# Another order for the mask work of a gated cross-attention block: vector engine, GpSimd and loads

## The reference

```python
q_in  = layernorm(x)
query = layernorm(q_in @ Wq + bq)            # 2 x 2048 x 512, 16 heads of 32
key, value = layernorm(ctx @ Wk + bk), layernorm(ctx @ Wv + bv)
scores = einsum('bhqd,bhkd->bhqk', query, key) / sqrt(32)
scores = where(mask[:, None] == 0, -1e9, scores)      # mask: 2 x 2048 x 154, int32
out = softmax(scores) @ value
x = x + tanh(g_xattn[1]) * (out @ Wo + bo)
```

## Time and profile before

| what | us |
|---|---|
| median of 3 runs | 2475.44 (2474.05 to 2477.65) |
| the profiled execution, its span from first to last instruction | 2475.2 |
| TensorE busy | 2414.1 (98%) |
| VectorE busy | 1444.5 (58%) |
| ScalarE busy | 1087.0 (44%) |
| GpSimd busy | 245.9 (10%) |
| DMA | 147.27 MB, mean 59 GB/s |

### The profile page before, as it was taken

How to read it: one execution, slowest core, us unless ns; L and a number is a source line. 1 busy time by engine, 2 the same in 40 slices (tenths; PEclk the granted TensorE clock), 3 DMA queues, 4 the chain that set the end, 5 groups by cost and what they waited for, 6 DMA issues and landing times.

```text
span 2475.2 us, 33128 instructions
## 1 busy us (share of the span) xinstructions
PE 2414.1 (98%) x13344; PEld 1826.1 (74%) x13344; DVE 1444.5 (58%) x2410; ACT 1087.0 (44%) x1762; POOL 245.9 (10%) x223
## 2 busy tenths in 40 slices
PE   6999999999999999999989999999999999999998
PEld 5666667688888888888755666666778888888886
DVE  5555566542222222222666666665888888888986
ACT  4343433442222222223334333334666666666665
POOL 2021112210000000000301111112000000000000
PEclk9999999999999999999999999999999999999999
DMA  3121111421101100102311222223501101101000
GB/s 126 35 86 52 52 52 69 158 85 52 52 1 52 51 18 35 51 18 85 113 58 61 78 78 78 78 73 102 167 18 35 52 18 48 38 20 49 35 30 22
DMA packets 92600, 147.27 MB, mean 59 GB/s; under 512 B 5408, under 2 KB 28320, under 8 KB 92448
## 3 DMA queue, kind: packets, MB, share of 16 engines
q1 hardware_dynamic: 92448, 145.16, 17.4%
HBM read 111.59 MB, written 33.55 MB: 59 GB/s over the span
## 4 chain that ended last, share of the span: by engine, by line
PE 40%; DVE 8%; ACT 2%; issue 1%; DMA 0%; POOL 0%; SPq 0%; DVEq 0%; ACTq 0%
PE l_lay_bank L69 18%; PE l_lay_score L69 11%; PE l_lay_values L1493 1%; PE l_lay_score L1416 1%; PE l_lay_score L1418 1%; PE l_lay_score L1468 1%; PE l_lay_values L1497 1%; PE l_lay_sums L1505 1%; DVE l_at_at_next L1036 1%; DVE l_at_h_lo L1050 1%; DVE l_at_at_next L1029 1%; DVE l_at_full L1025 1%; DVE l_at_full L1018 1%; DVE l_at_xTf_lo L924 1%; PE l_lay_bank L1339 1%
## 5 line engine op out<-in xcount | busy, mean ns | idle before, releaser
L69 PE MATMUL l_lay_score<-l_at_tw_hi,l_at_h_hi 128*128 128x512 f32 x1024 | 401.5, 392 | 5.2 <-DVE l_at_h_lo L1050 4.7
L69 PE MATMUL l_lay_bank<-l_at_xTf_hi,l_at_tw_hi 128*128 128x512 f32 x1024 | 400.0, 391 | 0.0
L69 PE MATMUL l_lay_score<-l_at_tw_hi,l_at_h_lo 128*128 128x512 f32 x1024 | 398.7, 389 | 0.0
L69 PE MATMUL l_lay_score<-l_at_tw_lo,l_at_h_hi 128*128 128x512 f32 x1024 | 398.5, 389 | 0.0
L69 PE MATMUL l_lay_bank<-l_at_xTf_hi,l_at_tw_lo 128*128 128x512 f32 x1024 | 398.4, 389 | 0.0
L69 PE MATMUL l_lay_bank<-l_at_xTf_lo,l_at_tw_hi 128*128 128x512 f32 x1024 | 398.4, 389 | 0.0
L1010 DVE TENSOR_TENSOR l_at_h_lo<-l_at_full,l_at_h_hi 128x512 fp32r<-128x512 f32 x128 | 99.6, 779 | 466.0 <-ACT l_at_h_hi L740 466.0
L735 ACT ACTIVATE l_at_full<-l_lay_bank,l_at_lay_b 128x512 f32<-128x512 f32 x128 | 88.4, 690 | 457.5 <-PE l_lay_bank L69 457.5
L69 PEld LDWEIGHTS l_lay_score<-l_at_tw_hi,l_at_h_hi 128*128 128x128 f32 x1024 | 192.2, 188 | 49.2 <-DVE l_at_h_lo L1050 10.3
L69 PEld LDWEIGHTS l_lay_score<-l_at_tw_hi,l_at_h_lo 128*128 128x128 f32 x1024 | 192.2, 188 | 40.3
L69 PEld LDWEIGHTS l_lay_bank<-l_at_xTf_hi,l_at_tw_lo 128*128 128x128 f32 x1024 | 192.2, 188 | 40.0
(11 more groups left out here) (224 smaller groups left out, 4078.9 us busy)
## 6 DMA issues: line engine op xcount, KB each, us to landing
both_x_in<-stream SPq DMA_DIRECT2D x25, 1024.0 KB, 5.6
l_at_xg<-stream SPq DMA_DIRECT2D x23, 1024.0 KB, 5.5
stream<-l_at_xg SPq DMA_DIRECT2D x22, 1024.0 KB, 4.3
l_at_tw_raw<-in_l_w SPq DMA_DIRECT2D x64, 256.0 KB, 5.6
l_at_maskT_in<-in_maskT SPq DMA_DIRECT2D x40, 256.0 KB, 2.6
both_x_in<-in_x SPq DMA_DIRECT2D x9, 1024.0 KB, 7.6
l_at_xg<-in_x SPq DMA_DIRECT2D x7, 1024.0 KB, 5.3
out<-l_at_xg SPq DMA_DIRECT2D x7, 1024.0 KB, 4.3
```

The lines of the kernel that those rows point to most:

```text
L69: done = nc.tensor.matmul(out, lhs[a], rhs[b], start=first and n == 0, stop=last and n == len(passes) - 1)
```

## The change

Only code under `norm`, that is layer 1, runs in another order; no instruction is added or removed. On VectorE, pieces 1 to 4 of chunk `it` are converted at the head of iteration `it` itself (1 and 2 between the halves of `xT_front`, 3 and 4 after `recip_of`), `mask_front` goes ahead of the query rows, piece 0 of the next chunk and the input norm between the query rows, the query norm directly behind its statistics, and `qT_front` one step later each. GpSimd takes `x_rstd_of` ahead of `q_rstd_of`. SP issues pieces 3 and 4 of chunk `it` at the start of iteration `it`, then the input, pieces 0 and 1 of the next chunk, the other mask, and piece 2. In the loops TensorE's and ScalarE's programs are as before.

```diff
--- before.py
+++ after.py
@@ -450,17 +450,20 @@
                 load_maskT(1, 0)
                 load_maskT(1, 1)
             for it in range(NCH):
+                if norm and it:
+                    load_maskT(it, 3)
+                    load_maskT(it, 4)
                 if it < last:
                     load(it + 2)
                 else:
                     load_last_residual()
-                if norm and it + 2 < NCH:
-                    load_masks(it + 2)
+                if norm and it:
+                    load_maskT(it + 1, 0)
+                    load_maskT(it + 1, 1)
                 if norm:
-                    for i in range(2, PIECES):
-                        load_maskT(it + 1, i)
-                    load_maskT(it + 2, 0)
-                    load_maskT(it + 2, 1)
+                    if it + 2 < NCH:
+                        load_masks(it + 2)
+                    load_maskT(it + 1, 2)
                 if it == last - 1:
                     weights(0)
                     weights(1)
@@ -588,10 +591,10 @@
                     add_bias(it - 1, gate_bias)
                 if it == last:
                     add_bias(last, gate_bias)
+                if it < last:
+                    x_rstd_of(it + 2)
                 if norm and it < last:
                     q_rstd_of(it + 1)
-                if it < last:
-                    x_rstd_of(it + 2)
                 if it:
                     widen(it - 1, range(RB, KT))
                 if it == last - 1:
@@ -1182,39 +1185,43 @@
                     if m in (8, 15):
                         kv_evict(6 + m // 15)
             for it in range(last):
-                xT_front(it + 1)
+                xT_front(it + 1, (0, 1))
+                if norm and it:
+                    maskT_front(it, 1)
+                    maskT_front(it, 2)
+                xT_front(it + 1, (2, 3))
                 if it:
                     recip_of(it - 1)
                 else:
                     k_lo_of(1)
-                for half in ((0, 1), (2, 3)):
-                    if norm:
-                        q_rows_front(it + 1, half)
-                    else:
-                        q_front(it + 1, half)
-                    if not norm and half[0] == 0:
-                        norm_stats(it + 2)
                 if norm:
+                    if it:
+                        maskT_front(it, 3)
+                        maskT_front(it, 4)
+                    mask_front(it + 1)
+                    q_rows_front(it + 1, (0, 1))
+                    maskT_front(it + 1, 0)
+                    norm_stats(it + 2)
+                    q_rows_front(it + 1, (2,))
+                    norm_apply(it + 2)
+                    q_rows_front(it + 1, (3,))
                     q_norm_stats(it + 1)
-                    norm_stats(it + 2)
                     q_norm_apply(it + 1)
                 else:
+                    q_front(it + 1, (0, 1))
+                    norm_stats(it + 2)
+                    q_front(it + 1, (2, 3))
                     norm_apply(it + 2)
                 if it:
                     c_back(it - 1, (0, 1))
                 if norm:
-                    mask_front(it + 1)
-                    maskT_front(it + 1, 0)
-                    norm_apply(it + 2)
-                    qT_front(it + 1, (0, 1))
+                    qT_front(it + 1, (0,))
                 if it:
                     c_back(it - 1, (2, 3))
                 for m in range(NM):
                     max_of(it + 1, m)
-                    if m in (2, 3) and norm:
-                        qT_front(it + 1, (m,))
-                    if m in (4, 6, 10, 13) and norm:
-                        maskT_front(it + 1, {4: 1, 6: 2, 10: 3, 13: 4}[m])
+                    if m in (1, 3, 5) and norm:
+                        qT_front(it + 1, ((m + 1) // 2,))
                     if it and m in (7, 11, 14):
                         y_back(it - 1, (m - 6) // 4)
                 if it:
@@ -1224,8 +1231,15 @@
                         v_normalise(2)
                         v_normalise(3)
                     front.take_lo(dve, "wd")
-            xT_front(NCH)
+            xT_front(NCH, (0, 1))
+            if norm:
+                maskT_front(last, 1)
+                maskT_front(last, 2)
+            xT_front(NCH, (2, 3))
             recip_of(last - 1)
+            if norm:
+                maskT_front(last, 3)
+                maskT_front(last, 4)
             for u in range(2):
                 if norm:
                     round_hidden(u)
```

## The result

| | before | after |
|---|---|---|
| median, us | 2474.74 (2473.79 to 2477.65, 4 runs) | 2538.55 (2537.29 to 2539.91, 4 runs) |
| ratio | | 1.0252 [1.0239, 1.0265] |
| profiled execution: span, us | 2475.2 | 2536.8 |
| TensorE's mean granted clock | 0.993 | 0.98 |

The changed kernel is 63.8 us slower. The forecast was 2533.0 (2492 to 2546), its likeliest case with a chance of 0.74; the median lies 5.6 us over it and inside the range. In the code after the change the same steps stand on other lines: the conversions on L919, `scores_main`'s first matmul on L1489, the maxima on L974 (VectorE) and L1430 and L1432 (TensorE), `qT_front`'s transposes on L1409, `add_bias` on L542.

A forecast was written before the change was run, and what follows sets the result against it. TensorE was taken to set the loop's pace. To the profiled span of 2475.2 us came 47.2 of mask waits and 11.9 of clock, less 1.35 at chunk 0: 2533.0 us, range 2492 to 2546.

The forecast's parts named there:

- likeliest case: Layer 1's chunks: mask pieces land behind the residual and `add_bias` delays their conversions; 2516 to 2545 us, chance 0.74.
- The loads behind the residual: SP, start of each iteration: pieces 3 and 4 land about 0.7 and 1.4 us behind the 1 MB residual.
- the hold: VectorE's conversion of piece 3 is held until GpSimd's running `add_bias` (4.6 us) ends; TensorE goes on 0.75 us later.
- the queue: Late landing behind the residual, conversions still 0.41 us: waits of 18.1 us; as a rival 2492 to 2504 us, chance 0.13.
- The rival of the overtaking pieces: Pieces 3 and 4 land after 2.6 us, before the residual; only chunk 1 waits, 2.2 us: 2476 us, chance 0.08.
- Chunk by chunk: TensorE's waits for the masks in chunks 1 to 7: 9.3, three of 4.7, two of 6.85, and 10.1 us.
- the second hold: Chunk 7: another `add_bias` follows at once and takes the ports between the two conversions; wait 10.1 us, otherwise 5.4.
- The clock: TensorE's clock falls once behind each of the 7 waits, 1.7 us each: 11.9 us, bounds 0 and twice that.
- VectorE's part: VectorE's new order in layer 1: 1.35 us gained at the end of chunk 0, nothing from its other moves.
- the first term: Four conversions leave the maxima loop of iteration 0, so TensorE gains 4 x 0.34 = 1.35 us.
- VectorE sets the pace: In the maxima loop of iteration 0 VectorE is the limit, so removing four conversions there saves TensorE 1.35 us.
- The sum: 2475.2 + 47.2 of waits - 1.35 at chunk 0 + 11.9 of clock = 2533.0 us.

The follow-up runs named there:

- experiment 2: The changed kernel with GpSimd's `add_bias` waiting until all masks of the chunk are converted, loads still behind the residual: 2501.18 us, ratio 1.0107.
- the swap alone: The kernel before with only GpSimd's `x_rstd_of` put ahead of `q_rstd_of`, VectorE's order unchanged: 2509.39 us, ratio 1.0131; 2509.74 us in a second set.
- experiment 1: The changed kernel with the next chunk's pieces 3 and 4 issued between the store and the residual load: 2476.14 us, ratio 1.0000.

## Why the prediction was right

**The loads behind the residual.** Right. The prediction had the pieces about 0.7 and 1.4 us behind the residual's landing. In chunk 1 the residual took 5.4 us from 1324.01 and the second piece 5.8 us from about 1324.9, 1.3 us behind it. With the hold gone the queue cost 17.4 us where 18.1 was worked out. The rival of the overtaking pieces fell: they would have landed after 2.6 us, and came ahead of the residual only once they were issued first (after 2.7 to 4.9 us). The chunks followed each other 69.3 to 76.3 us apart, where 67 and more was forecast.
The rule of the Trainium skill ("DMA: Bandwidth & Descriptors", "Queues, rings and completion order") that completion is not first in, first out gives no order; in these rows it was the order of issue.

**The hold.** Right, and the step with the least ground under it: one conversion of 1.34 us. The value taken, a hold to the end of `add_bias`, was the measured one: pairs of 4.47 to 4.50 us, and 4.15 us for the first conversion of chunk 7 where 0.41 is its own length. That it is `add_bias` that holds them is what experiment 2 shows.
The Trainium skill's exemption for one input in SBUF ("SBUF — State Buffer", "Who interferes with whom") did not apply to this instruction: 4.15 us. The same section names `tensor_scalar` among the operations that can enter a two-port mode, which the exemption leaves out. The rows fit that but don't prove it: the one from PSUM at 1763.26, of as many columns, takes 0.74 us, the conversion from SBUF 0.41.

**Chunk by chunk.** Forecast and measured waits: 9.3 and 8.95; 4.7 three times, and 4.80, 4.75, 5.17; 6.85 twice, and 6.57, 6.21; 10.1 and 10.95 with the second hold. The sum was 47.2 against 47.4. That the delay moves the next store and residual with it, so that the wait recurs, is what the seven rows show. The totals agree better than the parts, which is luck: chunk 7 is 0.85 over, and chunks 5 and 6 are 0.9 under. In chunk 7 the first `add_bias` began 1.5 us behind the place where TensorE needed the masks, not 0.1 as in the kernel before, and the second one took 4.67 us, not 5.04.

**The clock.** The mechanism was right, one fall at each of the seven waits, its size too small: 11.9 us forecast as 1.7 us a wait, 18.0 measured, within the bound of 23.8. Since the falls ahead of the waits are two here and three before, the clock term grew by 16.6 only; the prediction had no term for that. The 1.7 came from the fall behind a wait of 1.3 us; behind waits of 4.75 to 10.95 us it cost 1.6 to 3.3 us.

**VectorE's part.** "Nothing" held for everything but the first term. The four conversions that leave the loop over the maxima of chunk 0 were to give 1.35 us. VectorE's timeline of that loop after the change (first, the two places where it now stands idle, and what follows the loop):

```profile
1301.05 1.51 DVE L974 TENSOR_REDUCE l_at_maxes<-l_lay_score 128x4 f32<-128x616 f32 x2 [3.41 <-PE l_lay_score L1432]
...
1306.78 3.13 DVE L974 TENSOR_REDUCE l_at_maxes<-l_lay_score 128x4 f32<-128x616 f32 x4 [0.20 <-PE l_lay_score L1432]
1310.11 3.14 DVE L974 TENSOR_REDUCE l_at_maxes<-l_lay_score 128x4 f32<-128x616 f32 x4 [0.19 <-PE l_lay_score L1432]
1313.15 0.74 DVE L1109 SCALAR_TENSOR_TENSOR l_at_v_main<-l_at_v_main,l_at_lay_kv_mv,l_at_v_rows 128x512 f32<-128x512 f32 x1
```

The stretch takes 12.10 us, 12.86 before: a gain of 0.76. Without the conversions VectorE catches up with TensorE and waits 0.20 and 0.19 us for it, and the wait ahead of the first maxima grew from 1.3 to 1.8 us. The step that failed is "VectorE sets the pace": it did so only by a little.

**The sum.** Its start was off by chance. In all 97 executions here that have both numbers, the time lies 1.7 to 1.9 us over the span. So the profiled execution of before, with its span of 2475.2, took about 2477.0 us (an estimate), 2.3 over its median, and the 0.2 us between span and median were a coincidence. From the median instead, 2474.7 + 47.4 + 16.6 - 0.8 = 2537.9, 0.6 us short of the measured one. The 5.6 us between forecast and result are then -0.5 for the start, +0.2 for the waits, +4.7 for the clock, +0.6 for chunk 0, and 0.6 that are in no term.

## What to carry to other kernels

When a load is moved, look at what is issued just ahead of it on its queue, and at what starts on the other engines when that lands: here a residual of 1 MB was both the transfer in front and the trigger of the instruction that held the conversion. A small load with a near deadline goes ahead of the large one, into the time in which the queue waits anyway. Price each new wait of an otherwise busy TensorE at its length and, for waits from 3.4 us up as here, 1.6 to 3.3 us of clock on top, and treat a swap on a helper engine as free only together with the producer's order that it follows.

## What the runs showed of the hardware

- A conversion from int32 to bfloat16 with one input in SBUF was held by GpSimd's running instruction to its end (4.15 us in place of 0.41; without that instruction, beside the same transfers, 0.43 in experiment 2). Beside two GpSimd instructions back to back one conversion ended 0.3 us behind each: 4.15 and 4.71 us, 8.78 for the two.
- The clock's cost did not grow in step with the wait: behind six waits of 3.38 us (the swap alone) the falls cost 1.7 to 2.9 us each, 15.6 together; behind seven of 4.75 to 10.95 us they cost 1.6 to 3.3, 18.0 together. Both are 2.6 on average, since the time at 1.2 GHz within the wait itself (0.55 over 7 us of chunk 1's wait, with no matmul) costs nothing.
- A 256 KB load issued 0.4 to 1.0 us behind one of 1 MB landed after 5.7 to 6.8 us, and after 2.7 to 4.9 us when it was issued 1.6 us or more ahead of it (experiment 1).
